# Five columns and four in turn instead of four of 31: singles taken ahead of and behind the three columns that ScalarE marks

## The chip, the cores and the metric

The kernel runs on one NeuronCore of a Trainium2 chip. The metric is the device time of one execution in microseconds (us). TensorE multiplies matrices into PSUM, VectorE (DVE in the profile) and ScalarE (ACT) work on vectors, GpSimd (POOL) issues the indirect DMAs, and SyncE (SP) issues most other DMAs.

## The reference, cut to what matters

The reference is a graph network layer and a mixture of experts behind it. Two graph attention convolutions run on 6250 nodes with 8 heads of 16 channels; a feed-forward part of 8 experts, of which each node uses two, follows. The part that matters here is the first convolution over 200,000 random edges, ordered by target node, and 6,250 self loops:

```python
e = leaky_relu(a_s[src] + a_d[dst], 0.2)
m = segment_max(e, dst);  p = exp(e - m[dst]);  s = segment_sum(p, dst)
out = segment_sum(xw[src] * (p / s[dst])[:, :, None], dst)
```

For every edge the row of its source node is needed: 128 features and 8 scores, 136 floats (ROWT). The second convolution needs only the first 6250 entries of the edge list as its edges and is worked out before this part.

## The kernel before, in words

The edges behind the first 6272 lie as 128 partitions x 1563 columns. They are worked off in 51 batches of 31 columns (the last has 13). Three slots in SBUF (`G`) hold batches in turn.

For each column of a batch, 128 rows of the table `tables` must be fetched by index. GpSimd does it with one indirect DMA per column (`gather`, L935). In batches 7 to 49 (`by_pe`), the last four columns are not gathered. TensorE makes them: the table lies split in two parts in SBUF (`table_parts`), a one-hot matrix of 128 edges picks rows from 128 table rows at a time, and a matmul with 408 table values (three tiles of 136) in its moving operand fetches three candidates at once. There are 17 levels, so one column costs 17 x 2 = 34 matmuls (`product`, L1358) into one PSUM bank. `tile_pick` then says which of the three candidates counts.

The one-hots of the first three of the four columns are made by ScalarE in four stretches of levels (`mark_stretch`, L1214 and L1218): stretches 0 and 1 of the next batch while the features of the present one are copied back, stretches 2 and 3 in `batch_decays`, after L1169. Those of the fourth column are made by VectorE in one instruction (`mark_last_column`, L1829). TensorE's order for each batch is the four stretches of three columns (`columns`), then the fourth column (`last_column`). The four columns use PSUM banks 1, 5, 6 and 0.

VectorE's order for batch b is:

1. `take_columns(b)`: wait for all four columns, then three rows of four instructions (L1843, then L1845 twice), each picking one candidate for one column, with a drain after each row. The last lets TensorE begin the next batch (`columns_taken`).
2. `mark_last_column(b + 1)`.
3. `marks` (L1654 to L1660).
4. wait for the gathers of batch b, then `scan_batch` (from L1737): scores and running maxima, the differences for ScalarE's exponentials (L1745, L1756), the weighted features (L1758), and the scans along the columns (L1762, then eight times L1765), ended by L1770.

ScalarE copies the scanned features back into the slot in two halves (L1143, after four and after eight scans) and the remaining columns (L1183). SP then loads indices, target scores and codes of batch b + 3 and stores the slot (`fetch_and_store`, L681, L676, L690, L699); GpSimd begins gathering batch b + 3 into it when the store has landed.

The codes of the columns that TensorE makes (which level, which row of a tile) are worked out once after batch 1 (`code_columns`) and stored by SP at batch 2 with a transposing DMA of two-byte elements (L748). They are loaded for each batch, spread over all partitions (`fetch_codes`). At batch 4 SP loads the table (L745), which VectorE splits in batches 5 and 6 (`split_table`, L1859).

After the last batch GpSimd reads the last states of all nodes (`last_states2`, L974), waits for the slots to be stored, and reads and mends the rows at the borders of partitions (L944, L950); VectorE's L1958 uses the row of L944.

Of the kernel before, what the change touches and what calls it, by code (L numbers as in the profile page):

```python
# [24 lines left out]
ALU = mybir.AluOpType  # L25
# [3 lines left out]
P = 128  # L29
# [6 lines left out]
HD = 8  # L36
# [55 lines left out]
X_AT = {7: 4, 11: 5, 17: 6}  # L92
PEC = 4
PEA = 3
# [3 lines left out]
SPLIT_AT = 5  # L98
NPC = PEC * (PE1 - PE0)
LEV = 17  # L100
TPL = 3
# [8 lines left out]
assert NBLK * BLK == E and NG * GRP == NT and (NB + NA) % NS == 1 and sum(CO) == J1 and max(CO) * 2 * ROWS <= J * ROWS  # L110
assert CL + 1 <= WA and PEC < CL and 2 * HD * WA <= HL and 2 * ROWS * WA <= ROWS * L and ZT % ZJ == 0 and ZT * P == EP

# [5 lines left out]
def build(nc, x, src, dst, W0, as0, ad0, b0, W1, as1, ad1, b1, gamma, beta, Wg, bg, eW1, eb1, eW2, eb2, out):  # L118
    ctx = ExitStack()
    with ctx:  # L120
# [48 lines left out]
        table_parts = nc.alloc_sbuf_tensor_at("table_parts", [P, PARTS, part_size], rounded, offset=arena_at + 4 * XO, align_bytes=4)  # L169
        onehot = nc.alloc_sbuf_tensor_at("onehot", [P, LEV, PEC * P], rounded, offset=room_at, align_bytes=4)  # L170
        at = FB + PARTS * part_size - NT * D
        column_codes = [a.bitcast(code_type) for a in (AR[:, at:at + PEC * P // 2], room[:, CODES_AT:CODES_AT + PEC * P // 2])]
        assert at + PEC * P // 2 <= FB + 1152 and LEV * PEC * P <= CODES_AT and CODES_AT + PEC * P // 2 <= ROOM and LEV * TPL >= NT
        zero = room[:, 0:1024]
# [46 lines left out]
        src_code = tile_pick.rearrange("p n q -> p (n q)")[:, 0:NPC]  # L221
        code_out = room[:, NT * ROWT:NT * ROWT + NPC // 2].bitcast(code_type)
        minus_code = sb("minus_code", [P, LEV])
# [77 lines left out]
        columns_taken = sem("columns_taken")  # L301
        last_column_marked = sem("last_column_marked")
        last_column_used = sem("last_column_used")
        parts_ready = sem("parts_ready")
# [101 lines left out]
        def pe_columns(b):  # L406

            return PEC if by_pe(b) else 0

# [194 lines left out]
        def _(sp):  # L604
            with nc.allow_non_contiguous_dma(reason="small tables, once"):
# [124 lines left out]
                for b in range(NB):  # L730
# [18 lines left out]
                    if b == NB - 2:  # L749
                        sp.wait_ge(levels_used, len(STRETCHES) * (PE1 - PE0))  # L750
                        sp.wait_ge(last_column_used, PE1 - PE0)
# [109 lines left out]
        def _(pool):  # L861
# [118 lines left out]
            pool.wait_ge(levels_used, len(STRETCHES) * (PE1 - PE0))  # L980
            pool.wait_ge(last_column_used, PE1 - PE0)
            for n in range(4):
# [48 lines left out]
        def _(act):  # L1031
# [172 lines left out]
            def mark_stretch(b, i):  # L1204

                n, (first, end) = b - PE0, STRETCHES[i]
                if i == 0:
                    act.wait_ge(parts_ready, len(SPLITS))
                    act.wait_ge(codes_loaded[b % 2], 16 * (n // 2 + 1))
                if n >= 1:  # L1210
                    act.wait_ge(levels_used, len(STRETCHES) * (n - 1) + i + 1)
                for a in range(first, end):
                    v = LEVEL_ORDER[a]
                    last = S.activation(onehot[:, a, 0:PEA * P], column_codes[b % 2][:, 0:PEA * P], ACT.Abs, bias=minus_code[:, v:v + 1])  # L1214
# [99 lines left out]
        def _(pe):  # L1314
# [56 lines left out]

            def last_column(b):

                pe.wait_ge(last_column_marked, b - PE0 + 1)
                for a in range(LEV):
                    for k in range(PARTS):
                        mm = product(column_banks[PEA], onehot[:, a, PEA * P:PEC * P], a, k)
                mm.then_inc(last_column_used, 1)

# [111 lines left out]
        def _(dve):  # L1491
# [238 lines left out]

            def scan_batch(b, w=L, next_w=L):

# [91 lines left out]

            def mark_last_column(b):

                n = b - PE0
                dve.wait_ge(codes_loaded[b % 2], 16 * (n // 2 + 1))
                V.tensor_tensor(onehot[:, :, PEA * P:PEC * P], bc(column_codes[b % 2][:, PEA * P:PEC * P].unsqueeze(1), [P, LEV, P]),  # L1829
                                bc(own_code.unsqueeze(2), [P, LEV, P]), ALU.is_equal).then_inc(last_column_marked, 1)  # L1830

            def take_columns(b):

                dve.wait_ge(batch_stored[slot(b)], free_count(b))
                dve.wait_ge(levels_used, len(STRETCHES) * (b - PE0 + 1))
                dve.wait_ge(last_column_used, b - PE0 + 1)
                for q in range(TPL):
                    for c in range(PEC):
                        to = G[slot(b)][:, cols(b) - PEC + c, 0:ROWT]
                        n = PEC * (b - PE0) + c  # L1840
                        pick, of = tile_pick[:, n, q:q + 1], column_banks[c][:, q * ROWT:(q + 1) * ROWT]
# [4 lines left out]
                    if q == TPL - 1:  # L1846
                        last.then_inc(columns_taken, 1)
                    dd()

# [16 lines left out]
            def whole_batch(b, w=L, next_w=L):  # L1866
                if SPLIT_AT <= b < SPLIT_AT + len(SPLITS):
                    split_table(b - SPLIT_AT)
                if b == PE0 - 1:
                    own_codes()  # L1870
                    mark_last_column(PE0)
# [463 lines left out]
```

## Time and profile before

| | us |
|---|---|
| median of 3 runs | 3036.59 |
| lowest and highest | 3035.05, 3038.42 |
| the profiled execution, its own time | 3036.07 |
| its span in the profile | 3034.2 |
| busy in the span: PE, DVE, ACT, POOL | 2131.5, 2188.6, 1630.6, 1885.4 |

The page gives one row for a group of instructions of one line: how many, how long they were busy, the mean of one in nanoseconds, and the idle time of the engine just before them with what ended it. A busy share over the whole span says little here, since the expert stage (from about 2280 us) and the edge stage (from about 220 to 2005 us) are bound by different engines. The change is in the edge stage, and there in batches 7 to 49, from about 541 to 1971 us.

### The profile page before, as it was taken

What the parts mean: (1) busy time and instruction counts of PE and PEld (TensorE: products, weight loads), DVE (VectorE), ACT (ScalarE), POOL (GpSimd) and SP (SyncE); (2) the same over time, 40 slices, a digit from 0 to 9 for tenths busy, and PEclk for the clock granted to TensorE, in tenths of its full rate; (3) what the DMA queues carried; (4) which work ended last, traced back from release to release, by engine and by line L of the source; (5) the groups of instructions that cost most, each with busy time, mean ns of one, the idle gap of its engine ahead of it and who ended that gap; (6) DMA issues with size and microseconds to landing.
All of it is one profiled execution on the core that took longest, in us unless ns stands there. A gap on an engine that the chain in (4) does not pass through costs nothing.

```text
span 3034.2 us, 42972 instructions
## 1 busy us (share of the span) xinstructions
PE 2131.5 (70%) x11674; PEld 2015.1 (66%) x11675; DVE 2188.6 (72%) x4468; ACT 1630.6 (54%) x2613; POOL 1885.4 (62%) x1868
## 2 busy tenths in 40 slices
PE   4600002788887887888888888703449999999998
PEld 2400002787887787887878887603438999999997
DVE  7678877788887787888888887788864444444443
ACT  5424423687777776877777777624433333333332
POOL 5777767777777777777777777777771222222222
PEclk8855555898999898989998998855559999999999
DMA  9446993444444444444444444565772222222222
GB/s 357 135 145 179 159 239 123 127 127 143 147 128 127 140 150 127 127 152 139 128 127 147 143 127 127 167 218 168 260 257 37 38 37 37 38 38 37 38 37 31
DMA packets 278910, 395.04 MB, mean 130 GB/s; under 512 B 156236, under 2 KB 231569, under 8 KB 272257
## 3 DMA queue, kind: packets, MB, share of 16 engines
q1 hardware_dynamic: 202945, 244.92, 25.4%
q0 software_dynamic: 74000, 145.58, 20.9%
q10 hardware_dynamic: 1840, 3.06, 0.3%
q8 instruction: 55, 0.90, 0.1%
q14 instruction: 70, 0.57, 0.1%
HBM read 201.61 MB, written 191.79 MB: 130 GB/s over the span
## 4 chain that ended last, share of the span: by engine, by line
POOL 45%; PE 26%; issue 15%; DVE 7%; DMA 3%; ACT 2%; DVEq 2%; SPq 0%; POOLq 0%; ACTq 0%
POOL AR L935 43%; PE ps L1453 12%; PE ps L1459 12%; POOL placed L1003 1%; PE ps L1329 1%; DMA tables<-AR 1%; DVE group_stats L2020 1%; ACT AR L1262 1%; DVE AR L1718 1%; DVE AR L1765 1%; DMA state<-AR 1%; POOL AR L967 0%; DVEq L1760 0%; POOL room L974 0%; DVE AR L2144 0%
## 5 line engine op out<-in xcount | busy, mean ns | idle before, releaser
L935 POOL DMA_INDIRECT AR<-tables,idx x1391 | 1326.3, 954 | 425.6 <-issue 423.2
L1358 PE MATMUL ps<-table_parts,onehot 128*128 128x408 f32 (+1 forms) x5848 | 1202.1, 371 | 300.8 <-DVE AR L1845 161.2
L1358 PEld LDWEIGHTS ps<-table_parts,onehot 128*128 128x128 f32 x5848 | 1166.1, 209 | 336.9 <-DVE AR L1845 175.4
L1143 ACT COPY AR<-AR 128x1984 f32<-128x1984 f32 (+3 forms) x110 | 401.4, 3649 | 328.9 <-DVE AR L1765 286.2
L1012 POOL DMA_INDIRECT out<-AR,idb x105 | 184.0, 1753 | 568.5 <-issue 537.6
L1765 DVE TENSOR_TENSOR_SCAN AR<-ps,AR 128x512 f32<-128x512 f32 x404 | 454.2, 1196 | 0.0
L1453 PEld LDWEIGHTS ps<-AR 128*128 128x128 f32 x3360 | 393.0, 193 | 31.9 <-issue 26.6
L1453 PE MATMUL ps<-AR 128*128 128x128 f32 x3360 | 393.6, 276 | 26.5 <-DVE AR L2238 26.5
L1758 DVE TENSOR_TENSOR AR<-AR,ps 128x3968 f32<-128x3968 f32 (+1 forms) x51 | 356.6, 6991 | 0.0
L2238 DVE COPY AR<-AR 128x1024 f32 x210 | 151.1, 720 | 207.4 <-PE ps L1453 205.6
L1218 ACT ACTIVATE onehot<-onehot 128x1536 fp32r<-128x1536 f32 (+1 forms) x172 | 269.4, 1566 | 5.5
L1302 ACT ACTIVATE AR<-ps,bcur 128x128 f32<-128x128 f32 x424 | 121.2, 370 | 246.4 <-PE ps L1453 246.4
L1302 ACT ACTIVATE room<-ps,bcur 128x128 f32<-128x128 f32 x416 | 118.9, 369 | 242.4 <-PE ps L1453 242.3
L1214 ACT ACTIVATE onehot<-room,minus_code 128x384 fp32r<-128x384 f16 x374 | 198.7, 609 | 5.1 <-DVE table_parts L1862 5.1
L1459 PE MATMUL ps<-AR 128*128 x848 | 191.9, 379 | 1.3 <-DVE AR L2281 1.3
L1214 ACT ACTIVATE onehot<-AR,minus_code 128x384 fp32r<-128x384 f16 x357 | 189.5, 607 | 0.0
L1459 PE MATMUL ps<-AR,room 128*128 x832 | 188.2, 379 | 0.0
L1393 PE MATMUL ps<-ident,sml 128*128 128x128 f32 x6 | 2.4, 501 | 250.9 <-DVE sml L1922 250.9
L1459 PEld LDWEIGHTS ps<-AR 128*128 128x128 f32 x848 | 157.1, 190 | 20.9 <-issue 1.7
L1393 PEld LDWEIGHTS ps<-ident,sml 128*128 128x128 f32 x6 | 1.5, 311 | 251.9 <-DVE sml L1922 251.9
L1459 PEld LDWEIGHTS ps<-AR,room 128*128 128x128 f32 x832 | 154.1, 190 | 18.8
L1160 ACT ACTIVATE ps<-AR 128x248 f32<-128x248 f32 (+1 forms) x51 | 19.4, 380 | 259.9 <-DVE AR L1745 259.9
(345 smaller groups left out, 2456.7 us busy)
## 6 DMA issues: line engine op xcount, KB each, us to landing
state<-AR SPq DMA_DIRECT2D x50, 2232.0 KB
AR<-tables,idx POOLq DMA_INDIRECT x1440
AR<-in_L_ffn_W SPq DMA_DIRECT2D x16, 1024.0 KB
AR<-placed SPq DMA_DIRECT2D x420, 32.0 KB
AR<-adstart SPq DMA_DIRECT2D x50, 248.0 KB, 4.0
adstart<-room SPq DMA_DIRECT2D x21, 496.0 KB, 14.0
tables<-AR SPq DMA_DIRECT2D x49, 136.0 KB, 2.4
room<-tables SPq DMA_DIRECT2D x14, 476.0 KB, 4.2
```

The costliest lines, as they stand in the source:

```text
L935: pool.indirect_dma_start(out=G[s][:, j, 0:ROWT], out_offset=None, in_=table_rows, in_offset=bass.IndirectOffsetOnAxis(ap=idx[:, s, j:j + ...
L1012: pool.indirect_dma_start(out=out, out_offset=bass.IndirectOffsetOnAxis(ap=idb[:, s, :], axis=0), in_=ys[:, s, :], in_offset=None, bounds_ ...
L1143: return S.copy(to.rearrange("p j (h c) -> p j h c", h=HD)[:, :, :, a:z], of[:, :, 1:n + 1].rearrange("p (c h) j -> p j h c", h=HD)[:, :, ...
L1214: last = S.activation(onehot[:, a, 0:PEA * P], column_codes[b % 2][:, 0:PEA * P], ACT.Abs, bias=minus_code[:, v:v + 1])
L1218: S.activation(onehot[:, first:end, 0:PEA * P], onehot[:, first:end, 0:PEA * P], ACT.Relu, bias=1.0, scale=-1.0).then_inc(marked_by_act, 1)
L1302: last = S.activation(hsT[s][:, m, :], ps[2 * s + h][:, (m % 4) * P:(m % 4 + 1) * P], ACT.Gelu, bias=bcur[:, s, m:m + 1])
L1358: return T.matmul(bank[:, 0:z], mark, table_parts[:, k, v * w:v * w + z], start=(a == 0 and k == 0), stop=(a == LEV - 1 and k == PARTS - 1))
L1453: mm = T.matmul(ps[2 * s + h][:, m * P:(m + 1) * P], w1_cur[:, k, (h * 4 + m) * P:(h * 4 + m + 1) * P], xsT[:, s, k, :], start=(k == 0), s ...
L1459: mm = T.matmul(ps[5][:, 0:D], hsT[s][:, m, :], AR[:, bass.ds(e * (MH * D) + (NEX * KD * HID + m * D), D)], start=(m == 0), stop=(m == MH ...
L1758: V.tensor_tensor(TS[:, 0:F, js].rearrange("p (c h) j -> p c h j", h=HD), rows_in[:, :, 0:F].rearrange("p j (h c) -> p c h j", h=HD), bc(W ...
L1765: V.tensor_tensor_scan(T2[:, i * step:(i + 1) * step], decays(w), T2[:, i * step:(i + 1) * step], 0.0, ALU.mult, ALU.add).then_inc(entry_u ...
L2238: V.tensor_copy(w1_cur[:, :, h * 512:(h + 1) * 512], w1s[:, bass.ds(e, 1), :, h * 512:(h + 1) * 512].rearrange("p a k h -> p (a k) h")).th ...
```

## The change

TensorE makes five columns in batches 7, 9, ..., 49 and four in batches 8, 10, ..., 48. PEC, the number for which there are codes, is 5 for all batches. ScalarE marks the entries 1, 2 and 3 of the five. Entries 4 and 0 are singles: VectorE marks them, and both use the one-hot slice and the PSUM bank of the former fourth column. In a batch of four, entry 4 is the single and comes after the three columns, as the fourth column did. In a batch of five, TensorE makes entry 4 ahead of the three columns and entry 0 behind them. VectorE takes the first single of the next batch and marks the second in the middle of the eight scans of the present one. The three columns are now taken on their own wait, and `columns_taken` is given ahead of the take of the single behind them.

```diff
-PEC = 4
+PEC = 5
+SINGLES = (PE1 - PE0) + (PE1 - PE0 + 1) // 2
         def pe_columns(b):
-            return PEC if by_pe(b) else 0
+            return (PEC if takes_five(b) else PEC - 1) if by_pe(b) else 0
+        def takes_five(b):
+            return by_pe(b) and (b - PE0) % 2 == 0
+        def singles_ahead(b):
+            n = b - PE0
+            return n + (n + 1) // 2
...
# ScalarE, mark_stretch
-                    last = S.activation(onehot[:, a, 0:PEA * P], column_codes[b % 2][:, 0:PEA * P], ...)
+                    last = S.activation(onehot[:, a, 0:PEA * P], column_codes[b % 2][:, P:(PEA + 1) * P], ...)
...
# TensorE
-            def last_column(b):
-                pe.wait_ge(last_column_marked, b - PE0 + 1)
+            def single_column(nth):
+                pe.wait_ge(single_marked, nth + 1)
                 for a in range(LEV):
                     for k in range(PARTS):
                         mm = product(column_banks[PEA], onehot[:, a, PEA * P:(PEA + 1) * P], a, k)
+                mm.then_inc(single_used, 1)
...
             for b in range(PE0, PE1):
+                nth = singles_ahead(b)
+                if takes_five(b):
+                    single_column(nth)
                 for i in range(len(STRETCHES)):
                     columns(b, i)
-                last_column(b)
+                single_column(nth + takes_five(b))
...
# VectorE, scan_batch
                 for i in range(feature_scans(w)):
+                    if i == feature_scans(w) // 2:
+                        between()
                     V.tensor_tensor_scan(T2[:, i * step:(i + 1) * step], ...)
...
+            def take_single(b, e, nth):
+                dve.wait_ge(batch_stored[slot(b)], free_count(b))
+                dve.wait_ge(single_used, nth + 1)
+                take(b, (e,), (column_banks[PEA],))
+                dd()
+            def take_columns(b):
+                dve.wait_ge(batch_stored[slot(b)], free_count(b))
+                dve.wait_ge(levels_used, len(STRETCHES) * (b - PE0 + 1))
+                take(b, range(1, PEA + 1), column_banks).then_inc(columns_taken, 1)
+                dd()
+            def first_single_ahead(b):
+                if takes_five(b):
+                    take_single(b, PEC - 1, singles_ahead(b))
+                    mark_single(b, 0)
...
                 if by_pe(b):
                     take_columns(b)
+                    take_single(b, 0 if takes_five(b) else PEC - 1, singles_ahead(b) + takes_five(b))
                     if by_pe(b + 1):
-                        mark_last_column(b + 1)
+                        mark_single(b + 1, PEC - 1)
...
-                scan_batch(b, w, next_w)
+                scan_batch(b, w, next_w, lambda: first_single_ahead(b + 1))
```

`take` holds the picking instructions of the former `take_columns`, with a drain between its three rows; `mark_single(b, e)` is the former `mark_last_column` for entry e. SP and GpSimd wait for `single_used` at SINGLES, where they waited for `last_column_used`. `code_out` and the one-hot's width follow the new numbers; the one-hot stays as wide as it was.

## Rows read from the trace of the kernel before

**Rows 1.** The page's costliest groups: busy us, mean ns | idle before.

```profile
L935 POOL DMA_INDIRECT AR<-tables,idx x1391 | 1326.3, 954 | 425.6 <-issue 423.2
L1358 PE MATMUL ps<-table_parts,onehot 128*128 128x408 f32 (+1 forms) x5848 | 1202.1, 371 | 300.8 <-DVE AR L1845 161.2
```

**Rows 2.** The page's chain of waits, share of the span by line.

```profile
POOL AR L935 43%; PE ps L1453 12%; PE ps L1459 12%; POOL placed L1003 1%; PE ps L1329 1%; DMA tables<-AR 1%; DVE group_stats L2020 1%; ACT AR L1262 1%; DVE AR L1718 1%; DVE AR L1765 1%; DMA state<-AR 1%; POOL AR L967 0%; DVEq L1760 0%; POOL room L974 0%; DVE AR L2144 0%
```

**Rows 3.** Windows: length, busy us of each engine (count), granted clock, DMA share, GB/s.

```profile
541.60:1958.00 1416.40, 1172.90 (x5712) 1137.72 (x5712) 1181.88 (x1555) 1053.65 (x1171) 1070.87 (x1135) 0.90 0.43 136
1323.90:1327.30 3.40, 3.33 (x12) 3.27 (x13) 3.23 (x5) 3.37 (x5) 2.54 (x3) 0.50 0.38 94
```

**Rows 4.** Line L1843: ns min/median/max, first and last start us.

```profile
L1843 DVE TENSOR_SCALAR AR<-ps,tile_pick x172: 347/350/360, 541.6 to 1958.8; 128x136 f32<-128x136 f32 x172
```

**Rows 5.** Waits in 540:1960: us in total, times, longest.

```profile
DVE AR L1843 <- PE ps L1358: 142.1, 43, 5.4
...
PE ps L1358 <- ACT onehot L1218: 82.1, 36, 7.8
```

**Rows 6.** Timeline of one cycle: start us, us, engine, line [idle before <-releaser].

```profile
1320.29 1.16 DVE L1843 TENSOR_SCALAR AR<-ps,tile_pick 128x136 f32<-128x136 f32 x4 [4.29 <-PE ps L1358]
...
1321.52 2.39 DVE L1845 SCALAR_TENSOR_TENSOR AR<-ps,tile_pick,AR 128x136 f32<-128x136 f32 x8
...
1323.97 11.39 PE L1358 MATMUL ps<-table_parts,onehot 128*128 128x408 f32 x54 [3.82 <-DVE AR L1845]
1324.00 2.42 DVE L1829 TENSOR_TENSOR onehot<-room,ps 128x2176 fp32r<-128x2176 f16 x1
...
1328.36 0.58 DVE L1737 TENSOR_TENSOR AR<-AR,ps 128x248 f32<-128x248 f32 x1 [0.26 <-DMA AR<-tables,idx]
...
1335.29 1.48 ACT L1218 ACTIVATE onehot<-onehot 128x1536 fp32r<-128x1536 f32 x1
...
1336.83 15.38 PE L1358 MATMUL ps<-table_parts,onehot 128*128 128x408 f32 x82 [1.47 <-ACT onehot L1218]
...
1340.29 9.00 DVE L1765 TENSOR_TENSOR_SCAN AR<-ps,AR 128x512 f32<-128x512 f32 x8
...
1349.38 0.32 DVE L1770 COPY AR<-AR 128x144 f32<-128x144 f32 x1
...
1352.35 1.16 DVE L1843 TENSOR_SCALAR AR<-ps,tile_pick 128x136 f32<-128x136 f32 x4 [2.64 <-PE ps L1358]
...
1353.08 3.58 ACT L1143 COPY AR<-AR 128x1984 f32<-128x1984 f32 x1
```

**Rows 7.** Timeline of TensorE in four other places.

```profile
598.51 15.37 PE L1358 MATMUL ps<-table_parts,onehot 128*128 128x408 f32 x82 [1.07 <-ACT onehot L1218]
...
1018.13 12.32 PE L1358 MATMUL ps<-table_parts,onehot 128*128 128x408 f32 x54 [3.82 <-DVE AR L1845]
1036.18 17.34 PE L1358 MATMUL ps<-table_parts,onehot 128*128 128x408 f32 x82 [5.73 <-ACT onehot L1218]
...
1303.24 16.91 PE L1358 MATMUL ps<-table_parts,onehot 128*128 128x408 f32 x82 [3.47 <-ACT onehot L1218]
```

**Rows 8.** Timeline of VectorE: L1737 of batches 7 and 49.

```profile
556.11 0.58 DVE L1737 TENSOR_TENSOR AR<-AR,ps 128x248 f32<-128x248 f32 x1 [6.68 <-DMA AR<-tables,idx]
...
1971.08 0.57 DVE L1737 TENSOR_TENSOR AR<-AR,ps 128x248 f32<-128x248 f32 x1 [7.62 <-DMA AR<-tables,idx]
```

**Rows 9.** Timeline behind the last batch, GpSimd and VectorE.

```profile
1982.25 0.94 POOL L974 DMA_INDIRECT room<-state,node_index  x1 [0.30 <-issue]
...
2022.72 0.16 DVE L1958 TENSOR_TENSOR AR<-fix_row,ps 128x8 f32<-128x8 f32 x1 [2.08 <-DMA fix_row<-state,fix_index]
```

**Rows 10.** Timeline of SP and VectorE; landing of L748's DMA.

```profile
369.29 30.09 SPq L681 DMA_DIRECT2D idx<-srcp  x1
...
474.60 0.57 DVE L1737 TENSOR_TENSOR AR<-AR,ps 128x248 f32<-128x248 f32 x1 [9.25 <-DMA AR<-tables,idx]
...
DMA to landing us min/median/max: 59.7/59.7/59.7
```

More of the change, by code:

```diff
@@ L110 @@
 assert NBLK * BLK == E and NG * GRP == NT and (NB + NA) % NS == 1 and sum(CO) == J1 and max(CO) * 2 * ROWS <= J * ROWS
-assert CL + 1 <= WA and PEC < CL and 2 * HD * WA <= HL and 2 * ROWS * WA <= ROWS * L and ZT % ZJ == 0 and ZT * P == EP
+assert CL + 1 <= WA and PEC < CL and PE0 % 2 == 1 and 2 * HD * WA <= HL and 2 * ROWS * WA <= ROWS * L and ZT % ZJ == 0 and ZT * P == EP
 def bc(ap, shape):
@@ L169, in build @@
         table_parts = nc.alloc_sbuf_tensor_at("table_parts", [P, PARTS, part_size], rounded, offset=arena_at + 4 * XO, align_bytes=4)
-        onehot = nc.alloc_sbuf_tensor_at("onehot", [P, LEV, PEC * P], rounded, offset=room_at, align_bytes=4)
+        onehot = nc.alloc_sbuf_tensor_at("onehot", [P, LEV, (PEA + 1) * P], rounded, offset=room_at, align_bytes=4)
         at = FB + PARTS * part_size - NT * D
         column_codes = [a.bitcast(code_type) for a in (AR[:, at:at + PEC * P // 2], room[:, CODES_AT:CODES_AT + PEC * P // 2])]
-        assert at + PEC * P // 2 <= FB + 1152 and LEV * PEC * P <= CODES_AT and CODES_AT + PEC * P // 2 <= ROOM and LEV * TPL >= NT
+        assert at + PEC * P // 2 <= FB + 1152 and LEV * (PEA + 1) * P <= CODES_AT and CODES_AT + PEC * P // 2 <= ROOM and LEV * TPL >= NT
         zero = room[:, 0:1024]
@@ L221, in build @@
         src_code = tile_pick.rearrange("p n q -> p (n q)")[:, 0:NPC]
-        code_out = room[:, NT * ROWT:NT * ROWT + NPC // 2].bitcast(code_type)
+        code_out = room[:, NT * ROWT:NT * ROWT + NPC // 2 + 1].bitcast(code_type)[:, 0:NPC]
         minus_code = sb("minus_code", [P, LEV])
@@ L1213, in mark_stretch @@
                     v = LEVEL_ORDER[a]
-                    last = S.activation(onehot[:, a, 0:PEA * P], column_codes[b % 2][:, 0:PEA * P], ACT.Abs, bias=minus_code[:, v:v + 1])
+                    last = S.activation(onehot[:, a, 0:PEA * P], column_codes[b % 2][:, P:(PEA + 1) * P], ACT.Abs, bias=minus_code[:, v:v + 1])
                 last.then_inc(marked_by_act, 1)
@@ L1729, in keep_states, with scan_batch @@
                 V.tensor_copy(to[:, F:ROWS], of[:, F:ROWS])
-            def scan_batch(b, w=L, next_w=L):
+            def scan_batch(b, w, next_w, between):
                 q, s, n = NA + b, slot(b), cols(b)
@@ L1823, in own_codes, with mark_single, take @@
                 dd()
-            def mark_last_column(b):
+            def mark_single(b, e):
                 n = b - PE0
                 dve.wait_ge(codes_loaded[b % 2], 16 * (n // 2 + 1))
[L1829 to L1836, printed above, removed]
+                V.tensor_tensor(onehot[:, :, PEA * P:(PEA + 1) * P], bc(column_codes[b % 2][:, e * P:(e + 1) * P].unsqueeze(1), [P, LEV, P]),
+                                bc(own_code.unsqueeze(2), [P, LEV, P]), ALU.is_equal).then_inc(single_marked, 1)
+            def take(b, entries, banks):
                 for q in range(TPL):
[L1838 to L1841, printed above, removed]
+                    for e, bank in zip(entries, banks):
+                        to = G[slot(b)][:, cols(b) - PEC + e, 0:ROWT]
+                        n = PEC * (b - PE0) + e
+                        pick, of = tile_pick[:, n, q:q + 1], bank[:, q * ROWT:(q + 1) * ROWT]
                         if q == 0:
@@ L1845, in take_columns @@
                             last = V.scalar_tensor_tensor(to, of, pick, to, ALU.mult, ALU.add)
-                    if q == TPL - 1:
-                        last.then_inc(columns_taken, 1)
-                    dd()
+                    if q < TPL - 1:
+                        dd()
+                return last
+            def take_single(b, e, nth):
[7 more added lines that the diff above has]
+                take(b, range(1, PEA + 1), column_banks).then_inc(columns_taken, 1)
+                dd()
+            def first_single_ahead(b):
+                if takes_five(b):
+                    take_single(b, PEC - 1, singles_ahead(b))
+                    mark_single(b, 0)
             def split_table(k):
```

13 lines of the change are left out of this document (6 added, 7 removed).

## The prediction

> **What bounds the kernel now.** I read the page first, then the chain of waits, then who waited for whom in the stretch of the 43 batches that the diff touches (b = 7 to 49), then one cycle in the timeline. GpSimd's gathers (L935) are the largest group of the page [rows 1] and 43% of the chain [rows 2]. In the stretch 541.60:1958.00 GpSimd issues 1135 gathers in 1416.40 us, one per 1.248 us [rows 3], so a batch of 27 gathers takes 33.7 us. The reader should compare this with the cycle of the takes: L1843's first and last start [rows 4] give (1958.8 - 0.8 - 541.6) / 42 = 33.72 us (0.8 is the offset of the fourth instruction of a take). The cycle is GpSimd's. Yet the other loop is close behind. VectorE waits for TensorE 142.1 us in 43 takes, and TensorE stands 82.1 us for ScalarE's one-hots [rows 5], beside the 3.8 us in which each take holds it [rows 6]. In the cycle of [rows 6] from one take (1320.29) to the next (1352.35) VectorE waited 0.26 us for the gathers, and that cycle is 32.06 us. So a batch has only about 1.7 to 2 us between what the VectorE-TensorE loop needs and what GpSimd needs.
>
> **What goes.** 22 of the 43 batches (7, 9, ... 49) gather 26 columns, not 27: 22 x 1.248 = 27.5 us less for GpSimd. A pair of batches costs it 53 x 1.248 = 66.1 us against 67.4. This is all that the change can win, and only while GpSimd remains the bound.
>
> **What comes.** Per batch of five: 34 matmuls, one 2.42 us mark (as L1829), three picks. More important is the order. Both singles use one bank and one one-hot slice, so "take the single, then mark the next" stands in TensorE's path. I write the two kinds of cycle from one L1737 to the next, with these pieces of [rows 6]:
> - mark's end (1326.42) to L1737 without its wait: 1.68
> - L1737 to the third stretch marked by ScalarE (1336.77): 8.41
> - L1737 to the end of the scans (1349.71): 21.35
> - a pick is 0.35 [rows 4]; four take 1.16, so one more adds 0.27, and the next row of them starts 0.07 after the last. Three banks: 3 x (0.35 + 2 x 0.27 + 0.07) = 2.88. One bank: 3 x 0.42 = 1.26. No row shows a lone pick: 3 x 0.35 = 1.05 is the floor, and three of the length of L1737 (0.58 [rows 6]) give 1.74. I take 1.26, as its two parts are from the picks themselves.
> - mark: 0.09 + 2.42 = 2.51. Semaphore VectorE to TensorE 0.05 (1323.91 to 1323.97), TensorE to VectorE 0.14 (1352.21 to 1352.35).
> - a matmul at full clock: (15.37 - 0.37) / 81 = 0.185 us, 0.37 being its own length [rows 1, 7].
>
> Cycle A, TensorE on a batch of five: it stands idle until the first single is marked (0.14 + 1.26 + 2.51 + 0.05 = 3.96 us), then runs 170 matmuls. After the present idle time of 3.82 us the first 54 took 11.39 or 12.32 us instead of 10.2 [rows 6, 7], and the granted clock behind it is 0.50 for 3.4 us, the lower level of 1.2 GHz, where the whole stretch has 0.90 [rows 3]. The other 116 are 21.5 us. So 32.9 to 33.8; I take 33.2, as 11.39 is the usual value. A = 33.2 + 0.05 + 0.14 + 1.26 + 2.51 = 37.16 us (start and end both at a mark's end, so also from L1737 to L1737). VectorE's own work in A, 1.68 + 21.35 + 3.77 for the single and mark between the scans + 2.88 = 29.7, is hidden behind it. So is ScalarE: its second half copy began 3.8 us after the end of the eight scans (1353.08 against 1349.29 [rows 6]), and the pause in the scans is 3.8 too.
>
> Cycle B, TensorE on a batch of four: columns start with no idle time, since the three banks were taken beside the single. But the third stretch is marked only at L1737 + 8.41, and VectorE reaches L1737 1.26 + 2.51 + 1.68 behind the single. TensorE's first 54 matmuls end 3.9 us before that. Its last 82 took 15.37 us after a wait of 1.07, 16.91 after 3.47, 17.34 after 5.73 [rows 7]. I take 16.91. B = 8.41 + 0.05 + 16.91 + 0.14 + 1.26 + 2.51 + 1.68 = 30.96 us. If TensorE came back at full clock, VectorE would set B: 21.35 + 0.05 + 2.88 + 1.26 + 2.51 + 1.68 = 29.73.
>
> A + B = 68.1 us a pair. Ends: 32.9 with 29.73 gives 66.6; 33.8 with 17.34 gives 69.2; the picks (two on the path) add -0.4 or +1.0. So the pair is not below GpSimd's 66.1 at either end, and GpSimd runs ahead and waits. The gain in gathers is covered by a new bound that lies 0.7 us above the old 67.4.
>
> A rule of the Trainium skill bears on these lost microseconds ("TensorE: Matmul & The Clock Gate", "What's actually happening"): the low clock is the default and activity lifts it. The low granted clock behind TensorE's idle time agrees. Read for this change it is in favour, as TensorE works 306 matmuls a pair instead of 272; by it alone the pair would be near 66.6.
>
> **The sum.** Batch 7's L1737 stands at 556.11, waiting for its gathers [rows 8]; with one gather less it is 554.9. Batch 8 follows one B later, with the longer wait and 17.34: 31.4, so 586.3. Then 20 pairs, 1362.4, and one A, 37.2: batch 49's L1737 at 1985.9. Before it is at 1971.08, after a wait of 7.62 us for gathers [rows 8] that vanishes, as GpSimd is far ahead by then. That is +14.8 us. In the tail the fixing rows' gather waited behind GpSimd's 28 reads of states, which began at 1982.25 right behind the last gathers; VectorE waited 2.08 us for it [rows 9]. GpSimd is free as early as before while VectorE is later, so these 2.1 us go: +12.7.
> Against the profiled execution (3036.07, span 3034.2) this is 3048.8. The median of the runs, 3036.59, lies 0.5 above the profiled one: 3049.3, so 3049.
>
> **An edit outside the stretch.** The codes are stored in two-byte elements. NPC goes from 172 to 215, so 27,520 elements against 22,016. The store took 59.7 us to land and held SP's queue: L681 needed 30.09 us to issue [rows 10]. By count this grows by 14.9 us, and batch 5's slot, the kept rows and the table load behind them slip with it. I cost it at nothing: the slot's store is issued when L681 lets go, at 399.4, and VectorE is at batch 5's L1737 only at 474.60, after a wait of 9.25 us that a later table load can use up [rows 10]. Without that cover it costs up to 14.9.
> The Trainium skill ("DMA: Bandwidth & Descriptors", "Why a DMA increments its semaphore by 16 and not by 1") says that one descriptor moves one contiguous run. That speaks against the change: the count of descriptors grows by the same quarter; the row has only their total time.
>
> **The rivals.**
> - *GpSimd stays the bound or nearly (faster).* TensorE's loop comes in at 66.6 a pair, because the clock comes back at once in B and the shorter loss holds in A. Then 554.9 + 29.7 + 20 x 66.6 + 36.9 = 1953.5, 17.6 us before the old 1971.08, and 3036.6 - 17.6 - 2.1 = 3017. For it: a wait of 1.07 cost nothing. Against: 3.47 cost 1.5 us [rows 7], and mine is 3.9.
> - *No change.* After the wait for ScalarE TensorE loses time in half of the B cycles alone, VectorE setting the others at 29.73: pair 67.5, total 21 x 0.62 = 13 us less than forecast, 3036. For it: 15.37 and 16.91 lie only 2.4 us of wait apart.
> - *The codes' store reaches the path (slower still).* 3049 + 14.9 = 3064. It decides where batch 5's L1737 slips by more than 9.25 us or its gathers start later. For it: SP issues the slot's store and the adstart loads in order behind the codes. Against: the cover above.
> - *Five columns do not save gathers* is excluded: fetched_columns follows pe_columns.
>
> **Chances.** Forecast 0.55, clock returns 0.13, no change 0.17, codes' store 0.10, the rest (other mishaps) 0.05. The likeliest case's own range, from 67.6 a pair (a shorter pick and 32.9) to 68.8 (33.8 in half of the A cycles and 17.34 in B), is 3039 to 3063. A measurement here tells about 0.2% (6 us) from no change: faster means below 3030.5, slower above 3042.7. Faster 0.14; same 0.19 (the no-change case and a little of the forecast's low end); slower 0.67. Range 3028 to 3063: it leaves out most of the first rival and the top of the third.
>
> **What would show it.** Right: takes in pairs of 37 and 31 us instead of 33.7 each; GpSimd idle at L935 for DMA or SP instead of only "issue"; no wait of L1737 for gathers; TensorE idle for about 4 us ahead of each batch of five, released by the mark, and about 4 us for ScalarE inside each batch of four; granted clock near 0.9. Wrong: L935 still without idle time and a pair of 66.1; or batch 7's L1737 later than 556, which would be the codes' store.

## The result, and the profile after

The changed kernel took 3047.7 us (median of 7 runs, 3045.2 to 3048.3), the kernel before, run beside it, 3036.4 (7 runs): a ratio of 1.0037, interval 1.0025 to 1.0048. The change costs 11.3 us. The profiled execution took 3047.74 us, its span is 3045.9 (before 3036.07 and 3034.2).

L945 and L1368 are the former L935 and L1358, L1855 and L1857 the former L1843 and L1845, L1844 is the mark of a single, L1750 the former L1737. The page's groups and its chain of waits, against [rows 1, 2]:

```profile
L945 POOL DMA_INDIRECT AR<-tables,idx x1369 | 1307.6, 955 | 440.9 <-issue 413.7
L1368 PE MATMUL ps<-table_parts,onehot 128*128 128x408 f32 (+1 forms) x6596 | 1298.4, 361 | 227.4 <-DVE onehot L1844 134.9
...
PE ps L1368 33%; PE ps L1466 12%; PE ps L1472 12%; POOL AR L945 8%; DVE onehot L1844 3%; DMA tables<-AR 1%; ACT onehot L1224 1%; DVE AR L1857 1%; ACT onehot L1228 1%; POOL placed L1013 1%; PE ps L1339 1%; DVEq L1773 1%; DVE group_stats L2053 1%; DVE AR L1780 1%; ACT AR L1272 1%
```

22 gathers are gone. GpSimd's share of the chain fell from 43% to 8%, and TensorE's matmuls of one-hots stand there with 33%. The same chain, cut to 560:1980 us and summed by line, shows the loop that now sets the time: TensorE, VectorE's mark, ScalarE's one-hots, the picks.

```profile
by line: PE ps L1368 71.5%; DVE onehot L1844 7.0%; ACT onehot L1224 2.9%; ACT onehot L1228 2.1%; DVE AR L1857 2.1%; issue 1.9%; POOL AR L945 1.1%; DVE ps L1756 1.0%; DVE AR L1855 1.0%; ACT ps L1179 0.8%; DVEq L1671 0.8%; DVEq L1751 0.7%; DV
```

Who waited for whom in 540:1960, as [rows 5] (us in total, times, longest):

```profile
POOL AR L945 <- issue: 338.4, 1109, 0.6
...
DVE AR L1855 <- PE ps L1368: 113.7, 41, 3.3
...
PE ps L1368 <- ACT onehot L1228: 91.3, 21, 5.5
PE ps L1368 <- DVE onehot L1844: 83.9, 22, 4.2
POOL AR L945 <- DMA state<-AR: 24.9, 11, 4.2
DVE AR L1750 <- DMA AR<-tables,idx: 8.1, 2, 6.6
```

TensorE stands twice a pair: 83.9 / 22 = 3.8 us for the mark ahead of five, 91.3 / 21 = 4.3 us for ScalarE inside four. GpSimd waits for slots to be stored, and VectorE waited for gathers only twice. Both waits of TensorE are in the timeline of one pair, against [rows 6]; first TensorE's rows (the last one ends with the view), then VectorE's:

```profile
1266.96 42.35 PE L1368 MATMUL ps<-table_parts,onehot 128*128 128x408 f32 x224 [3.89 <-DVE onehot L1844]
1313.55 17.73 PE L1368 MATMUL ps<-table_parts,onehot 128*128 128x408 f32 x82 [4.25 <-ACT onehot L1228]
1335.17 37.11 PE L1368 MATMUL ps<-table_parts,onehot 128*128 128x408 f32 x196 [3.89 <-DVE onehot L1844]
```

```profile
1268.49 0.58 DVE L1750 TENSOR_TENSOR AR<-AR,ps 128x248 f32<-128x248 f32 x1
...
1299.79 0.36 DVE L1855 TENSOR_SCALAR AR<-ps,tile_pick 128x136 f32<-128x136 f32 x1 [3.33 <-PE ps L1368]
1300.22 0.79 DVE L1857 SCALAR_TENSOR_TENSOR AR<-ps,tile_pick,AR 128x136 f32<-128x136 f32 x2
...
1301.09 2.42 DVE L1844 TENSOR_TENSOR onehot<-AR,ps 128x2176 fp32r<-128x2176 f16 x1
...
1305.10 0.57 DVE L1750 TENSOR_TENSOR AR<-AR,ps 128x248 f32<-128x248 f32 x1
...
1331.39 0.36 DVE L1855 TENSOR_SCALAR AR<-ps,tile_pick 128x136 f32<-128x136 f32 x1 [2.38 <-PE ps L1368]
...
1336.71 0.59 DVE L1750 TENSOR_TENSOR AR<-AR,ps 128x248 f32<-128x248 f32 x1
```

From L1750 to L1750 cycle A is 1305.10 - 1268.49 = 36.61 us and cycle B 31.61.

The granted clock of TensorE in the stretch of [rows 3], and right behind the two waits (length, then busy us by engine, then the clock):

```profile
541.60:1958.00 1416.40, 1239.99 (x6295) 1217.99 (x6295) 1240.66 (x1620) 1048.66 (x1164) 1055.31 (x1118) 0.92 0.44 136
...
1313.55:1317.00 3.45, 3.45 (x10) 3.36 (x11) 3.38 (x3) 3.42 (x5) 2.82 (x3) 0.50 0.27 61
1331.28:1335.17 3.89, 0.00 (x1) 0.00 (x0) 3.55 (x5) 3.89 (x5) 2.98 (x4) 1.00 0.24 54
1335.20:1338.60 3.40, 3.40 (x12) 3.36 (x13) 3.03 (x8) 2.54 (x4) 2.52 (x3) 0.60 0.94 185
```

VectorE's L1750 of batches 7, 8, 48 and 49, against [rows 8]:

```profile
549.90 0.58 DVE L1750 TENSOR_TENSOR AR<-AR,ps 128x248 f32<-128x248 f32 x1 [1.49 <-DMA AR<-tables,idx]
...
588.57 0.59 DVE L1750 TENSOR_TENSOR AR<-AR,ps 128x248 f32<-128x248 f32 x1 [6.59 <-DMA AR<-tables,idx]
...
1951.05 0.58 DVE L1750 TENSOR_TENSOR AR<-AR,ps 128x248 f32<-128x248 f32 x1
...
1985.32 0.56 DVE L1750 TENSOR_TENSOR AR<-AR,ps 128x248 f32<-128x248 f32 x1
```

The row of 1331.28 is the idle time ahead of the first single: the clock still stood at 1.00 in it and fell only when TensorE had begun again.

A pair is (1951.05 - 588.57) / 20 = 68.12 us; before, the same reckoning gives 67.20. Batch 49 stands 14.24 us later than before (1971.08), and the rest of the span is 1060.6 us against 1063.1: 14.2 - 2.5 = 11.7, which is all of the difference of the two profiled executions.

### The profile page after: what moved, and what is told of

Read it like the earlier page. It is cut to its first block, busy times and chain, and to the rows that moved or that the text cites. A ratio compares the mean times of both kernels' runs of the same rounds, so it can differ in the third digit from the quotient of the medians.

```text
span 3045.9 us, 44794 instructions
## 1 busy us (share of the span) xinstructions
PE 2226.8 (73%) x12422; PEld 2124.9 (70%) x12423; DVE 2272.1 (75%) x4556; ACT 1638.0 (54%) x2613; POOL 1863.8 (61%) x1846
## 4 chain that ended last, share of the span: by engine, by line
PE 59%; DVE 14%; POOL 10%; issue 5%; ACT 4%; DVEq 4%; DMA 2%; SPq 1%; POOLq 0%; ACTq 0%
PE ps L1368 33%; PE ps L1466 12%; PE ps L1472 12%; POOL AR L945 8%; DVE onehot L1844 3%; DMA tables<-AR 1%; ACT onehot L1224 1%; DVE AR L1857 1%; ACT onehot L1228 1%; POOL placed L1013 1%; PE ps L1339 1%; DVEq L1773 1%; DVE group_stats L2053 1%; DVE AR L1780 1%; ACT AR L1272 1%
## 5 line engine op out<-in xcount | busy, mean ns | idle before, releaser
L945 POOL DMA_INDIRECT AR<-tables,idx x1369 | 1307.6, 955 | 440.9 <-issue 413.7
L1368 PE MATMUL ps<-table_parts,onehot 128*128 128x408 f32 (+1 forms) x6596 | 1298.4, 361 | 227.4 <-DVE onehot L1844 134.9
L1368 PEld LDWEIGHTS ps<-table_parts,onehot 128*128 128x128 f32 x6596 | 1275.3, 201 | 250.6 <-ACT onehot L1228 98.6
L1153 ACT COPY AR<-AR 128x1984 f32<-128x1984 f32 (+3 forms) x110 | 408.9, 3718 | 332.3 <-DVE AR L1780 289.5
```

What stands on the lines that cost most here:

```text
L945: pool.indirect_dma_start(out=G[s][:, j, 0:ROWT], out_offset=None, in_=table_rows, in_offset=bass.IndirectOffsetOnAxis(ap=idx[:, s, j:j + ...
L1153: return S.copy(to.rearrange("p j (h c) -> p j h c", h=HD)[:, :, :, a:z], of[:, :, 1:n + 1].rearrange("p (c h) j -> p j h c", h=HD)[:, :, ...
L1368: return T.matmul(bank[:, 0:z], mark, table_parts[:, k, v * w:v * w + z], start=(a == 0 and k == 0), stop=(a == LEV - 1 and k == PARTS - 1))
```

## The experiments

All times are medians beside runs of the kernel before on the same chip. These had medians of 3036.7 us (gathers27, before26, fill_a, fill_b), 3038.1 (mid_half, mid_34, mid_all, codes_more), 3036.8 (fill_ab) and 3040.1 (mix_34, mix_23). Pairs are from L1750 (whatever its line in a run) of batch 8 to that of batch 48, over 20. The edits are cut to what matters; for the orders of the single VectorE's part of the edit is left out.

### gathers27: are the gathers off the path?

```diff
+                if takes_five(b):
+                    pool.indirect_dma_start(out=spare[...], in_=adstart, in_offset=...idx[:, s, J - PEC:J - PEC + 1]...)
                 for j in range(fetched_columns(b)):
```

> The changed kernel, with the 22 saved gathers issued again: ahead of each batch of five GpSimd fetches one more indexed column (16 floats a row from adstart) into a tile that nobody reads. GpSimd then needs 54 x 1.248 = 67.4 us a pair, as before the change. Theory (the VectorE-TensorE loop of 68.1 us a pair is the bound): no change against the changed kernel, 3048 +- 3 us, GpSimd's idle time at the gathers shrinking from 26.9 us towards nothing. Rival (the relief of GpSimd is still worth its 27.5 us and something else costs more): 3075 us.

3049.5 us, ratio 1.0041 (1.0027 to 1.0055), a pair 68.21. With 22 gathers issued again (of shorter rows than the saved ones, 16 floats) the time is that of the changed kernel, within 2 us. The waits of its GpSimd in 540:1960 are "issue" but for 0.3 us, the wait for stored slots is gone, and VectorE never waits for gathers from batch 8 to batch 48:

```profile
POOL AR L953 <- issue: 340.1, 1116, 0.3
```

So the change bought GpSimd only idle time.

### before26: is the gain there if TensorE's loop stays as it was?

```diff
-            return cols(b) - pe_columns(b)
+            return cols(b) - pe_columns(b) - (1 if by_pe(b) and (b - PE0) % 2 == 0 else 0)
```

> The kernel before with one part of the change alone: in batches 7, 9, ..., 49 GpSimd gathers 26 columns, and the 27th is left as it lies in the slot (its edges are wrong in the output), while TensorE and VectorE still make four. Theory: the old loop needs 31.7 us a batch when nothing holds it, GpSimd 66.1 us a pair, so GpSimd stays the bound and the whole saving of 22 x 1.248 = 27.5 us shows: 3009 to 3012 us. Rival (GpSimd was not the bound, or the gathers' transfers are): less than 10 us of gain, 3027 or more.

This kernel leaves the 27th column of every second batch out. 3009.6 us, ratio 0.9908 (0.9892 to 0.9923), a pair 66.06: GpSimd's 53 x 1.248 = 66.1. The saved gathers are worth 27.2 us where nothing is added. The fifth column's work turns that into a loss of 11.

### fill_a: what does the clock cost behind the mark?

```diff
+            def filler(count):
+                for _ in range(count):
+                    T.matmul(column_banks[0][:, 0:TPL * ROWT], table_parts[:, 0, 0:P], table_parts[:, 0, 0:TPL * ROWT], start=True, stop=True)
                 if takes_five(b):
+                    if b > PE0:
+                        pe.wait_ge(columns_taken, b - PE0)
+                        filler(19)
                     single_column(nth)
```

> The changed kernel, with 19 spare matmuls of 128x408 (3.5 us) ahead of the first single of each batch of five from batch 9 on, into the bank of the first column, which the next real matmul there clears. They lie in the time in which TensorE waits for VectorE's take and mark. Theory (TensorE loses 1 to 2 us behind that wait to the lower granted clock): cycle A falls from 36.6 to about 35.6, 21 x 1.0 = 21 us less, 3027 us. Rival (the loss is a start-up cost of the stall and not of the clock, or the spare matmuls delay the single): 3048 us or more.

3008.4 us, ratio 0.9908 (0.9892 to 0.9923), where 3027 was expected: nearly twice the foreseen gain. TensorE in one pair (start, length, count, wait):

```profile
1290.97 18.01 PE L1368 MATMUL ps<-table_parts,onehot 128*128 128x408 f32 x82 [4.26 <-ACT onehot L1228]
1308.82 3.67 PE L1385 MATMUL ps<-table_parts 128*128 128x408 f32 x19
1312.87 40.79 PE L1368 MATMUL ps<-table_parts,onehot 128*128 128x408 f32 x224 [0.38 <-DVE onehot L1852]
1357.91 16.91 PE L1368 MATMUL ps<-table_parts,onehot 128*128 128x408 f32 x82 [4.25 <-ACT onehot L1228]
```

The same 224 useful matmuls take 40.79 us instead of 42.35, although TensorE begins them no earlier. The pair fell from 68.12 to 66.30, that is 1.82 x 21 = 38 of the 39 us gained. Of it A gave 1.55 (36.6 to 35.05) and B the rest. I had expected less, since [rows 6] have 11.39 us for the first 54 matmuls, 1.2 more than the 10.2 that I took for full speed. The two rows of 224 differ by 1.56, and B gave something too. The granted clock of 560.00:1940.00 is 0.96. Behind the same wait of 4.25 for ScalarE the 82 matmuls took 18.01 and 16.91 us by turns, so the length of the wait alone doesn't fix what it costs. The clock tells the three cases apart (the changed kernel with 17.73 first, then fill_a with 18.01 and with 16.91):

```profile
1313.55:1318.75 5.20, 5.20 (x15) 5.06 (x16) 5.13 (x4) 3.46 (x5) 3.98 (x5) 0.50 0.24 54
1290.97:1296.75 5.78, 5.78 (x17) 5.62 (x18) 5.71 (x5) 3.46 (x5) 4.51 (x5) 0.50 0.25 60
1358.30:1361.60 3.30, 3.30 (x12) 3.20 (x11) 3.23 (x3) 3.07 (x5) 2.51 (x3) 0.50 0.26 62
```

The matmuls ran at the lower clock for 5.2, 5.8 and 3.3 us, and lost 2.4, 2.6 and 1.5 us against the 15.37 of full speed: roughly half of that time each.

### fill_b: and behind ScalarE's one-hots?

```diff
                 for i in range(len(STRETCHES)):
+                    if i == 2 and not takes_five(b):
+                        pe.wait_ge(single_marked, nth + 1)
+                        filler(column_banks[PEA], 19)
                     columns(b, i)
```

> The changed kernel, with 19 spare matmuls (3.5 us) between the second and third stretch of each batch of four, where TensorE waits about 4.2 us for ScalarE's one-hots; they go to the singles' bank, ahead of the single that clears it. Theory: the last 82 matmuls fall from 17.7 to 15.4 us and VectorE becomes the limit of cycle B at 29.7 instead of 31.6 us; pair 66.3, just over GpSimd's 66.1; 21 x 1.9 = 40 us less, 3008 to 3012 us. Rival (the loss is not the clock's): 3048 us.

3015.6 us, ratio 0.9931 (0.9918 to 0.9945).

```profile
1291.67 3.68 PE L1385 MATMUL ps<-table_parts 128*128 128x408 f32 x19
1296.10 15.37 PE L1368 MATMUL ps<-table_parts,onehot 128*128 128x408 f32 x82 [0.75 <-ACT onehot L1228]
1315.70 43.19 PE L1368 MATMUL ps<-table_parts,onehot 128*128 128x408 f32 x224 [4.24 <-DVE onehot L1852]
```

Now the 82 take 15.37 us, full speed, and B is mostly 29.6 to 29.7 us, VectorE's own sum of the prediction (29.73). But A rose to between 36.4 and 37.9, so the pair was 66.62 and the kernel missed the foreseen 3008 to 3012. The clock behind the wait of 4.24 points at the reason, 0.50 for 5.3 us, where in the changed kernel it was low for less than 3.5 (1335.90:1339.20 has 0.50, 1339.35:1367.00 has 1.00):

```profile
1315.70:1321.00 5.30, 5.29 (x16) 5.17 (x17) 4.74 (x12) 5.27 (x9) 4.08 (x5) 0.50 0.50 126
```

Whether all of A's rise is the clock or a part is work that the shorter B moves was open, hence the next.

### fill_ab: both pauses filled

The two edits above together.

> Both fillings together: 19 spare matmuls ahead of the first single of a batch of five and 19 between the second and third stretch of a batch of four; nothing else differs from the changed kernel. Alone, the first took cycle A from 36.6 to 35.05 us and left B at 31.4 (alternating 30.8 and 32.0); the second took B to 29.6 and let A rise to 36.5 to 37.8. Theory: all of this is the granted clock behind TensorE's pauses (A's rise in the second is a dearer recovery after the one pause left). Then with both pauses filled A is 35.0 and B 29.6, the loop needs 64.7 a pair, GpSimd's 66.1 is the bound again, VectorE waits for gathers, the granted clock of the stretch is 0.99 or 1.00, and the time is within 3 us of 3006 (as the first filling, 66.30 a pair, less 21 x 0.2). Rival: A's rise comes from work that the second filling moves (ScalarE's or VectorE's order behind a shorter B), not from the clock. Then A stays at 36.5 or more less 1.55, that is 35.0 to 36.3, and B at 29.6: 64.6 to 65.9 a pair, and the two are told apart by A's matmuls: 170 in 31.5 us by the theory, and idle time of TensorE inside A by the rival. Were the spare matmuls not free but cost their own 3.7 us anywhere, the pair would be above 68.

3009.4 us, ratio 0.9911 (0.9895 to 0.9928), a pair 66.12. TensorE in one place, the window 560.00:1940.00, and the waits in 560:1960:

```profile
1357.53 15.37 PE L1368 MATMUL ps<-table_parts,onehot 128*128 128x408 f32 x82 [0.75 <-ACT onehot L1228]
1373.24 3.79 PE L1385 MATMUL ps<-table_parts 128*128 128x408 f32 x19 [0.34 <-DVE AR L1868]
1377.13 31.16 PE L1368 MATMUL ps<-table_parts,onehot 128*128 128x408 f32 x170
```

```profile
560.00:1940.00 1380.00, 1332.43 (x7151) 1297.47 (x7151) 1254.57 (x1624) 1056.87 (x1159) 1043.25 (x1106) 1.00 0.43 137
```

```profile
DVE AR L1761 <- DMA AR<-tables,idx: 63.3, 24, 6.3
```

The clock is 1.00, the 170 matmuls of five columns take 31.16 us instead of 32.7, and VectorE waits for gathers again: GpSimd is the bound, and this is no faster than fill_a, which had reached it. So A's rise in fill_b was the clock: the 82 matmuls of B are as fast here, and the rise is gone. The changed order of TensorE with no lost clock would gain all that GpSimd gives. The time is 0.4 us above the foreseen 3003 to 3009, within what the measurement tells.

### mid_half, mid_34, mid_all: another order

The single of a batch of four, or the first of five, goes between the second and third stretch, where TensorE waited for ScalarE. VectorE takes it between the scans. mid_half keeps five in every second batch with the first single ahead of its columns; mid_34 has five in 33 of 43 and mid_all in all, with the first single in the middle of each and none ahead.

```diff
                 for i in range(len(STRETCHES)):
+                    if i == 2:                        # mid_half: and not takes_five(b)
+                        single_column(nth)
                     columns(b, i)
-                single_column(nth + takes_five(b))
+                if takes_five(b):
+                    single_column(nth + 1)
...
-            return by_pe(b) and (b - PE0) % 2 == 0
+            return by_pe(b) and (b - PE0) % 4 != 3    # mid_34; mid_all: by_pe(b)
```

> The changed kernel with the single of a batch of four moved: TensorE makes it between the second and third stretch of that batch, in the time in which it waited for ScalarE, and VectorE takes it in the middle of the scans of the batch before, and there marks the first single of the next batch of five. No take and mark then stands ahead of a batch of five, and the wait for ScalarE is filled with work. Theory: by the same durations the VectorE-TensorE loop needs 29.7 + 33.4 = 63.1 us a pair, so GpSimd with 66.1 is the bound again and the 27.5 us show: 3008 to 3012 us, as in the run with 26 gathers and four columns. Rival (five and four columns cost the loop more than GpSimd's 66.1 wherever the single stands): 3030 us or more.

3007.8 us, ratio 0.9906 (0.989 to 0.9921), a pair 66.27: again GpSimd's. VectorE waited for gathers, 63.0 us in 28 times in 560:1900. The order alone, with no spare work, wins back what the fillings did. It does not end TensorE's pauses, as one of about 3 us for ScalarE is left in each batch of five,

```profile
PE ps L1368 <- ACT onehot L1228: 63.3, 20, 5.4
```

and the clock of 560:1940 is 0.96, not 1.00. But no take and mark stands ahead of a batch of five any more, and the loop with what it loses stays under GpSimd's 66.1.

> The same order with the first single of every batch between the second and third stretch, and five columns in three batches of four (33 of the 43). GpSimd needs (3 x 26 + 27) x 1.248 / 4 = 32.76 us a batch, VectorE by its instructions (3 x 33.4 + 29.7) / 4 = 32.5, TensorE 170 matmuls or 31.5 us at full clock. Theory: GpSimd bound by a hair, 33 x 1.248 = 41 us less than the kernel before: 2995 to 3000 us. Rival (TensorE loses more to the lower clock or the two loops do not nest): 3010 us or more.

3011.2 us, ratio 0.991 (0.9895 to 0.9925), where 2995 to 3000 was expected: a clear miss. TensorE where a five follows a four, and its largest waits in 560:1900:

```profile
1316.58 57.75 PE L1368 MATMUL ps<-table_parts,onehot 128*128 128x408 f32 x306 [8.23 <-DVE AR L1858]
```

```profile
PE ps L1368 <- DVE AR L1858: 106.4, 30, 8.5
DVE AR L1856 <- PE ps L1368: 33.8, 13, 3.3
```

A four in this order leaves TensorE with nothing to do until the three columns are taken: 8.23 us idle, where the single ahead of five would stand. The cycle up to that four's scans (the former L1737, L1751 here) is 29.6 us, but the one from there on is 36.7, and those of fives behind fives are 33.3. In sum (two of 33.3, 36.7, 29.6) that is 66.5 a pair.

> The same order with five columns in all 43 batches. GpSimd needs 32.4 us a batch, VectorE 1.68 + 21.35 + 3.77 + 2.88 + 3.77 = 33.45. Theory: VectorE is the bound at 33.4 to 33.5, hardly under the 33.7 of the kernel before, so 3018 to 3026 us. Rival (GpSimd sets the time): 43 x 1.248 = 54 us less, 2983 us.

3017.6 us, ratio 0.9934 (0.9919 to 0.9949), just under the foreseen 3018: the cycles are 33.3 to 33.7 us, the clock 1.00, and from batch 8 on VectorE never waits for gathers. Here VectorE is the bound, as foreseen (33.45). With five columns in every batch its own work is longer than GpSimd's 26 x 1.248 = 32.4.

### mix_34 and mix_23: the mix that mid_34 and mid_all point to

The edit against mid_34:

```diff
+                ahead = takes_five(b) and b > PE0 and not takes_five(b - 1)
+                if ahead:
+                    single_column(nth)
                 for i in range(len(STRETCHES)):
-                    if i == 2:
+                    if i == 2 and not ahead:
                         single_column(nth)
```

A five behind a four makes its first single ahead, all other batches in the middle. mix_34 has five in 33 batches, mix_23 in 29 (two of three).

> Five columns in three batches of four, as in the run before, but a batch of five behind one of four has its first single ahead of its three columns (TensorE stood idle there for 8.2 us, until VectorE had taken the four's columns), the others have it between the second and third stretch. Theory: the cycle into such a batch falls from 36.7 to 33.3 us, the mean VectorE cycle is (3 x 33.3 + 29.6) / 4 = 32.4, and GpSimd with 32.76 us a batch is the bound: 10 x 3.3 us less than before, down to 2995 to 2999 us. Rival (GpSimd and VectorE, 0.4 us apart, hold each other up): 3003 us or more.

2999.0 us (2998.7 to 2999.6), ratio 0.9863 (0.9846 to 0.9879), at the upper end of the foreseen 2995 to 2999. This beats both kernels, by 41 us the one before. The 8.23 us became 2.29:

```profile
1328.63 32.87 PE L1368 MATMUL ps<-table_parts,onehot 128*128 128x408 f32 x170 [2.29 <-DVE onehot L1848]
1362.72 6.44 PE L1368 MATMUL ps<-table_parts,onehot 128*128 128x408 f32 x34 [1.22 <-DVE onehot L1848]
1370.33 25.12 PE L1368 MATMUL ps<-table_parts,onehot 128*128 128x408 f32 x136 [1.18 <-DVE AR L1861]
```

A pair is 65.59 us, VectorE waited for gathers 11.0 us in all, and the granted clock is 0.99. GpSimd's (3 x 26 + 27) x 1.248 / 2 = 65.52 a pair is the bound, and VectorE's cycles of 33.3 and 29.6, 64.8 a pair, lie close below it.

> The same with five columns in two batches of three (29 of the 43). GpSimd needs 32.88 us a batch, VectorE (2 x 33.3 + 29.6) / 3 = 32.1. Theory: GpSimd bound with more room to spare, 29 x 1.248 = 36 us less than the kernel before: 2999 to 3003 us. Rival: the switches between four and five, more frequent here, cost more than the room: 3006 us or more.

3004.2 us (3003.3 to 3005.3), ratio 0.988 (0.9863 to 0.9896), some 1 us above what was expected, and 5.2 behind mix_34: four fives less leave 4 x 1.248 = 5.0 us of gathers.

### codes_more: what does the codes' store cost?

```diff
                         sp.dma_start(codes.rearrange("c p -> p c"), code_out).then_inc(lists_stored, 16)
+                        sp.dma_start(more_codes.rearrange("c p -> p c"), code_out[:, 0:86]).then_inc(more_stored, 16)
```

> The changed kernel with one more store of two-byte elements behind that of the codes: 86 x 128 elements, twice what the change added, into memory that nobody reads, waited for ahead of the table load. By the change's own 11.5 us for 5504 elements it holds SP's queue 23 us longer. Of this 1.1 (a wait at the table) has already shown, and VectorE's waits of 5.6, 6.6 and 1.5 us for the gathers of batches 5 to 7 can take up to 13.7: 5 to 17 us more than the changed kernel, 3053 to 3065 us. If the store lies off the path altogether: 3048 us.

(The load of the table waits for this store too.) 3062.9 us, ratio 1.0083 (1.0069 to 1.0097), 15.2 us above the changed kernel; each against the kernel before beside it, 24.8 against 11.3. The timeline of SP, ScalarE and VectorE:

```profile
345.82 63.80 SPq L762 DMA_DIRECT2D more_codes<-room  x1
...
409.66 24.77 SPq L693 DMA_DIRECT2D idx<-srcp  x1
...
448.10 3.55 ACT L1204 ACTIVATE room<-AR,nmr,rstd 128x256 f32<-128x256 f32 x7 [24.81 <-DMA hbd<-room]
...
451.68 2.02 DVE L2020 TENSOR_TENSOR room<-room,ps 128x1792 f32<-128x1792 f32 x1 [28.83 <-ACT room L1204]
```

SP's queue is held for 63.80 + 24.77 = 88.6 us. The rows that ScalarE normalises for the later stage are stored by the same queue (`hbd`), ScalarE waited 24.81 us for such a store before it could fill the buffer again, and VectorE 28.83 us for ScalarE, where the same instruction of the changed kernel (L2016 there) had waited 4.94, and batch 5's L1754 stands at 493.38 instead of 473.61. The changed kernel itself, with one store, reads (timeline of SP and VectorE)

```profile
370.05 41.55 SPq L691 DMA_DIRECT2D idx<-srcp  x1
...
458.07 1.08 DVE L1891 TENSOR_SCALAR room<-room 128x1768 int32<-128x1768 int32 x1 [1.12 <-DMA room<-tables]
...
473.61 0.57 DVE L1750 TENSOR_TENSOR AR<-AR,ps 128x248 f32<-128x248 f32 x1 [5.59 <-DMA AR<-tables,idx]
```

The hold of 41.55 us is nearly covered: the table came 1.12 us too late for its split, and VectorE still had 5.59 us to wait for gathers at batch 5 (9.25 before). So a longer hold does reach the path, in a place that the prediction had not named. The size is no confirmation of the prediction's 14.9 us or of this run's own reckoning: the queue was held 47 us longer than in the changed kernel, where 23 were expected by count of elements, and that 15.2 us came out inside the foreseen 5 to 17 is partly luck.

## Why the prediction was right, by its steps

- **What bounds it.** That GpSimd was the bound, and by more than the 0.6 us a batch that the change takes from it, is confirmed by before26: 22 gathers fewer are worth 27.2 us, the 27.5 of the prediction.
- **Cycle A**, forecast 37.16, measured 36.61. TensorE's idle time is 3.89 (3.96), the 170 matmuls took 32.72 (33.2), just under the low end of my bounds (32.9). That end was 11.39 + 21.5, by the usual start; the 33.2 that I took is 0.3 more than the reason given for it yields. And full speed was reckoned too slow: fill_ab has 31.16 for 170 where my 10.2 + 21.5 make 31.7. The loss behind the pause was 1.6 us, more than the 1.2 of the first 54.
- **Cycle B**, forecast 30.96, measured 31.61. Up to the third stretch it fits: 1313.55 - 1305.10 = 8.45 (8.46 with the semaphore), and from the end of the matmuls to L1750 1336.71 - 1331.28 = 5.43 (0.14 + 1.26 + 2.51 + 1.68 = 5.59). The term that was mis-sized is TensorE's: 82 matmuls took 17.73 us where I had put 16.91, behind a wait of 4.25. [Rows 7] had 16.91 behind 3.47 and 17.34 behind 5.73. The measured value lies above both, so my upper bound was none.
- **The pair** came out at 68.12, as forecast, because the two errors are about equal with opposite signs (-0.55 and +0.65); the mean holds one short first cycle of 33.69 behind batch 8's wait, and from batch 10 on it is 68.27. That the sum hit is luck; that neither end of the bounds came below GpSimd's 66.1 was the argument, and it held.
- **The clock rule.** The rival of 3017 needed the clock back at once. The rows show 0.50 and 0.60 in the 3.4 us behind the two waits (0.50 is the lower level, 1.2 GHz; the 0.60 is 1.00 at first and then 0.50), and fill_ab shows that with the pauses filled the same order runs at 1.00 and gives 3009. The Trainium skill ("TensorE: Matmul & The Clock Gate", "What's actually happening") has the low clock as the default which activity lifts; the runs agree: more matmuls made the kernel 39 us faster. What the prediction drew from it for this change, near 66.6 a pair, did not come: the clock of the stretch rose from 0.90 to 0.92 alone, and the pair was 68.12. The 34 matmuls more a pair counted for little while two pauses of 4 us stayed.
- **The start.** Batch 7 stood at 549.90 instead of 554.9, but batch 8 waited 6.59 us for its gathers, which I had not foreseen, and stood at 588.57 instead of 586.3. In gathers27 batch 7 waited 6.73 us for its gathers and stood at 557.8, and batch 8 waited for none and stood at 588.57 all the same. Why the gathers of batch 8 (there of batch 7) came so late is not shown. This step was off by +2.3 us.
- **The last cycle.** The sum ended with a whole A of 37.2 us, but from batch 48 to 49 it is 1985.32 - 1951.05 = 34.27. Batch 50 has no column of TensorE's, so no mark (0.09 + 2.42) stands in that cycle; the prediction overlooked this. Its -2.9 us cancel the +2.3 of the start, which is luck again, and brought batch 49 to 1985.32 against the forecast 1985.9.
- **The codes' store.** L691 held SP for 41.55 us against 30.09, 11.5 more instead of 14.9, and was covered, as costed. codes_more shows that a longer hold reaches the path.
- **The tail.** Forecast -2.1, measured -2.5. The wait for the fixing rows is gone: VectorE's instruction that uses them (the former L1958) began at 2034.98 without one.
- **No change** (3036) needed B cycles at full clock in half of the cases. 18.01 and 16.91 by turns in fill_a show that the loss can alternate, though not with none; in the changed kernel both kinds of cycle were steady.

So the likeliest case held as a mechanism: gathers27 says that GpSimd is off the path, before26 that the gain was there, the fillings that the loop would fall under GpSimd's 66.1 but for TensorE's lower clock behind its pauses, and mid_half that an order without the take and mark ahead of a batch of five keeps the gain too.

The 17.73, 16.91 or 18.01 us of 82 matmuls behind the same wait of 4.25 us, and the 1.6 us that 170 lose behind 3.89, go with how long the clock stayed low under them (see fill_a). What stays open is why it stayed low for 5.2 us in one place and for 3.3 in another.

## What to carry to other kernels

Work taken from the bound engine pays only up to the next loop, so sum up that loop wait by wait before the move: here 27 us of gathers were given away for a new wait of about 4 us on TensorE in every second cycle, and the slow matmuls behind it. Where a single resource (one bank, one one-hot slice) puts "take, mark, multiply" in a row, look first for a place in which the consumer waits anyway; putting the single there won 40 us over the change with the same columns on TensorE. And an idle TensorE costs twice, in the pause and in the slow stretch behind it.

## What the runs showed of the hardware

Matmuls that compute nothing made the kernel faster: 19 of them, 3.67 us in each second batch, took 39.3 us off (3047.7 to 3008.4). In mix_34, 136 matmuls behind 1.18 us of idle time took 25.12 us, 0.185 each, which is full speed. Behind 2.29 us 170 took 32.87, behind 3.89 us in the changed kernel 32.72, and behind almost none in fill_ab 31.16. Behind 8.23 us in mid_34, 306 took 57.75, where 31.16 for 170 and 25.12 for 136 make 56.28. The loss behind a pause of 2 us or more lay between 1.5 and 2.6 us in TensorE's rows of this part and did not grow with the pause: 1.5 behind 8.23, 2.6 behind 4.26. It went with the time at the granted clock of 0.50, which began in one place in the pause (1309.30:1313.55 has 0.81) and in another only behind it (1331.28:1335.17 has 1.00).
